# Attention with heads of 8: rounds of two steps, and each half of a step's scores issued beside a unit of the other row half

## What is computed

```python
qc, kc, vc = heads(x @ Wcq + bcq), heads(ctx @ Wck + bck), heads(ctx @ Wcv + bcv)   # 16 heads of 8
attc = einsum('bhqd,bhkd->bhqk', qc, kc) * 8 ** -0.5                                # 256 x 1601 per head
y = einsum('bhqk,bhkd->bhqd', softmax(att_causal), v)                               # first layer only
y = y + einsum('bhqk,bhkd->bhqd', softmax(attc), vc)
x = x + y.reshape(B, T, 128) @ Wp + bp                                              # input is layernorm(x)
```

## Time and profile before

| | |
|---|---|
| median of 3 runs | 7738.05 us (7690.1 to 7750.57) |
| span of the profiled execution | 7680.6 us |
| TensorE (PE) busy | 6854.6 us, 89% |
| VectorE (DVE) busy | 5897.9 us, 77% |
| ScalarE (ACT) busy | 4972.7 us, 65% |
| GpSimd (POOL) busy | 2316.8 us, 30% |
| L688, exponentials, 5248 of them | 2821.1 us busy |
| L747, reductions of wide units, 4608 of them | 3053.5 us busy |
| L625, pv, 20992 matmul records | 1615.8 us busy |

### The profile page before, as it was taken

One profiled execution on the slowest core, in us unless ns is written; L12 is line 12 of the kernel. 1 busy time (PEld: TensorE's weight loads), 2 busy tenths in 40 slices (PEclk: granted clock), 3 DMA queues, 4 the chain that ended last, 5 costly groups with the idle time before them and its releaser, 6 DMA issues. The chain is left out here.

```text
span 7680.6 us, 186325 instructions
## 1 busy us (share of the span) xinstructions
PE 6854.6 (89%) x73814; PEld 3108.2 (40%) x73814; DVE 5897.9 (77%) x12885; ACT 4972.7 (65%) x9846; POOL 2316.8 (30%) x2368
## 2 busy tenths in 40 slices
PE   6999999977999998788769999999996889999979
PEld 2333333343333333344424444444444433333335
DVE  6888888846898997788757777777774488999955
ACT  4787788834888886455446666666653168888842
POOL 1222222111211210155435555555554112212100
PEclk9999999987999999899879999999998589999989
DMA  5344444104434341100100000000001144343400
GB/s 101 86 98 94 94 91 94 44 27 84 95 78 103 81 92 44 28 18 17 40 22 10 9 8 10 6 10 9 5 5 56 28 103 99 75 103 85 85 26 12
DMA packets 319830, 417.82 MB, mean 54 GB/s; under 512 B 56533, under 2 KB 238054, under 8 KB 318969
## 3 DMA queue, kind: packets, MB, share of 16 engines
q1 hardware_dynamic: 317432, 405.36, 23.2%
q10 hardware_dynamic: 1536, 0.53, 0.0%
HBM read 225.41 MB, written 174.66 MB: 52 GB/s over the span
## 5 line engine op out<-in xcount | busy, mean ns | idle before, releaser
L688 ACT ACTIVATE a_probs<-scores_ps 128x512 f32<-128x512 f32 (+2 forms) x5248 | 2821.1, 591 | 356.9 <-PE scores_ps L608 263.7
L747 DVE TENSOR_REDUCE a_unit_max<-bank 128x1 f32<-128x512 f32 x3072 | 2003.7, 683 | 180.2 <-PE bank L595 145.3
L625 PE MATMUL bank<-a_probs,a_v_sb 128*9 128x256 f32 (+1 forms) x20992 | 1615.8, 380 | 29.3 <-ACT a_out_sb L695 20.3
L1299 ACT ACTIVATE cross_probs<-scores_ps 128x512 f32<-128x512 f32 (+1 forms) x1792 | 868.6, 571 | 590.4 <-PE scores_ps L1194 590.4
L608 PE MATMUL scores_ps<-a_stack 64*128 64x256 bf16 (+1 forms) x10496 | 1131.7, 275 | 60.9 <-ACT a_probs L688 55.9
L1381 DVE TENSOR_REDUCE cross_unit_max<-bank 128x1 f32<-128x512 f32 x1536 | 979.2, 685 | 253.3 <-PE bank L1180 250.2
L747 DVE TENSOR_REDUCE a_unit_max<-scores_ps 128x1 f32<-128x512 f32 x1536 | 1049.8, 683 | 160.4 <-PE scores_ps L595 143.1
L595 PE MATMUL bank<-a_stack 63*128 63x512 bf16 (+2 forms) x3413 | 1039.7, 372 | 7.4 <-DMA a_stack<-a_stack_dram 2.1
L1465 POOL TENSOR_TENSOR cross_added<-cross_probs 128x1024 f32<-128x1024 f32 x384 | 905.6, 2358 | 327.3 <-PE bank L1227 241.5
L608 PEld LDWEIGHTS scores_ps<-a_stack 64*128 64x128 bf16 (+1 forms) x10496 | 373.3, 96 | 991.1 <-ACT a_probs L688 831.7
L512 POOL CAST a_parts<-a_qk 128x512 bf16<-128x512 f32 (+3 forms) x225 | 117.7, 523 | 1893.8 <-ACT a_qk L707 1814.2
(11 more groups left out here) (421 smaller groups left out, 10031.3 us busy)
## 6 DMA issues: line engine op xcount, KB each, us to landing
a_stack_dram<-a_parts SPq DMA_DIRECT2D x288, 400.2 KB, 4.3
a_stack<-a_stack_dram SPq DMA_DIRECT2D x256, 348.2 KB, 8.0
a_stack<-a_stack_dram SPq DMA_DIRECT2D x128, 444.2 KB, 9.9
a_ctxT<-in_ctxT SPq DMA_DIRECT2D x48, 400.2 KB, 4.8
a_stack_dram<-a_parts SPq DMA_DIRECT2D x288, 64.0 KB, 2.4
a_stack_dram<-a_parts SPq DMA_DIRECT2D x96, 128.0 KB, 2.4
f_x<-x_after_dram SPq DMA_DIRECT2D x32, 256.0 KB, 3.3
x_after_dram<-a_res SPq DMA_DIRECT2D x48, 128.0 KB, 4.3
```

Of the source, the lines that this page charges most:

```text
L625: ins = pe.matmul(out_bank[32 * h:32 * h + V8, q0:TOK], v[0:n, e.t, 4 * e.g + h, :], A.probs[0:n, held, o + q0:o + TOK], start=(e.t == 0), ...
L688: act.activation(by_pair(A.probs[0:n, b, a * 512:(a + 1) * 512])[:, :, q0:TOK], by_pair(score_bank[(2 * e.i + a) % 3][0:n, :])[:, :, q0:TO ...
L747: ins = dve.tensor_reduce(unit_max[:, e.g % 2, qt, 2 * a + j, c:c + 1], bank[:, 0:e.s.chunks[c][1]], AX.X, ALU.max)
L1299: act.activation(probs[0:n, b, h, 0:m, :].rearrange("p m q -> p (m q)"), score_bank[h][0:n, 0:m * TOK], ACT.Exp, scale=scale).then_inc(S[" ...
```

## The change

Plan: `segment8`, which wrote one batch at a time, is replaced by `plan8`, which writes all batches in one list, in rounds of two steps. A round is, in order: scores half 0 of the even step, its exponential, its first units, the emptying of a side job of the round before (`late`), scores half 1, its exponential, its units, one side job of the kind `first` with its emptying (k_cross, v_cross), the same two halves for the odd step, then the pv of the two steps before the round (and of the even step too if it ends a quad), then `rest` (GpSimd's splits, transfers, layer norm), then at most one side job of the kind `last`, whose emptying is `late` in the next round. Window starts move by two steps (`SPACE8` 4 to 6). Units alternate their row half the other way round (`k ^ 1`), and the first unit of a half is issued between that half's two scores matmuls. `negmax` has two buffers. Scores of a half wait only for the bank of that half.

```diff
+    def evac(n, place, e):
+        done = put(n, place, "evac", e.batch)
+        done.job = e
+    def first(n, kind, b, **k):
+        e = put(n, "first", kind, b, **k)
+        evac(n, "first", e)
+    def last(n, kind, b, **k):
+        n += n % 2
+        while n in taken:
+            n += 2
+        taken[n] = kind
+        e = put(n, "last", kind, b, **k)
+        evac(n + 2, "late", e)
+        return n
...
+            n = last(stop, "turn", b, s=s, g=g)
+            put(n + 2, "late", "row", b, s=s, g=g)
...
+        for c in range(len(cross.chunks)):
+            first(ahead + 2 * c, "k_cross", b, c=c)
+            put(ahead + 2 * c, "rest", "split", b, j=c)
+        put(ahead, "rest", "ln_stats", b)
+        put(ahead, "rest", "ln_rstd", b)
+        put(ahead + 2, "rest", "ln_apply", b)
+        n = last(ahead + 4, "x_turned", b)
+        n = last(n + 2, "q", b)
...
+            first(ahead + 10 + 2 * j, "v_cross", b, j=j)
...
+            n = last(max(n + 2, done - done % 2 + 2 * (done % 2 == 0)), "quad_out", b, quad=quad)
...
+        n = last(n + 4, "heads_turned", b)
+        last(n + 2, "proj", b)
+
+    for n0 in range(-end, max(n for n, _ in at) + 2, 2):
+        core = 0 <= n0 < total
+        for half in range(2):
+            n = n0 + half
+            units = units_at.get(n, [])
+            for a in range(2):
+                mine = units[a * len(units) // 2:(a + 1) * len(units) // 2]
+                if core:
+                    s, g, t = steps[n % end]
+                    plan += [Ev("scores", s=s, g=g, t=t, i=n, part=a), Ev("exp", s=s, g=g, t=t, i=n, part=a)]
...
+                    if mine and mine[0].s.row_tile(mine[0].k) != a:
+                        plan[-2].beside = mine[0]
+                        mine[0].woven = True
+                plan += mine
+                if half == 0 and a == 0:
+                    plan += at.get((n0, "late"), [])
+            if half == 0:
+                plan += at.get((n0, "first"), [])
+        if 0 <= n0 <= total:
+            upto = n0 + int(n0 < total and steps[n0 % end][2] == steps[n0 % end][0].T - 1)
+            for i in range(gone, upto):
+                s, g, t = steps[i % end]
+                plan.append(Ev("pv", s=s, g=g, t=t, i=i))
...
+            gone = max(gone, upto)
+        plan += at.get((n0, "rest"), []) + at.get((n0, "last"), [])
```

TensorE's program:

```diff
-                    if e.i >= 1:
-                        pe.wait_ge(S["probs"], 2 * e.i - 1)
+                    a = e.part
+                    if 2 * e.i + a >= 3:
+                        pe.wait_ge(S["probs"], 2 * e.i + a - 2)
...
                     for j in range(2):
-                        for a in range(2):
-                            ins = pe.matmul(score_bank[(2 * e.i + a) % 3][0:n, j * TOK + q0:(j + 1) * TOK],
...
+                        ins = pe.matmul(score_bank[(2 * e.i + a) % 3][0:n, j * TOK + q0:(j + 1) * TOK],
...
+                        if j == 0 and e.beside:
+                            unit(e.beside)
```

More of the change, by code:

```diff
@@ L39 @@
 V8 = 9
-LAG8 = 3
 def key_tiles(nk):
@@ L243, in segment8 @@
[L243 to L253, removed]
@@ L256, in segment8, with put @@
-    if with_next:
-        for c in range(len(cross.chunks)):
[L258 to L264, removed]
+    total = BATCH * end
+    at, units_at, taken = {}, {}, {}
+    def put(n, place, kind, b, **k):
+        e = Ev(kind, **k)
+        e.batch = b
+        at.setdefault((n // 2 * 2, place), []).append(e)
+        return e
@@ L278, in segment8 @@
[L278 to L297, removed]
@@ L298, in segment8 @@
-    for e in plan:
-        e.cur = cur
-        e.batch = cur - 1 if e.kind in ("pv", "quad_out") and e.nxt else cur + 1 if e.nxt else cur
+            last(ahead + 18, "v_own", b)
+        done = base
+        n = base
+        for quad in range(QUADS * len(sources)):
+            done += sources[quad // QUADS].T
+            n = last(max(n + 2, done - done % 2 + 2 * (done % 2 == 0)), "quad_out", b, quad=quad)
+        put(base + end, "rest", "x_res", b)
+        n = last(n + 4, "heads_turned", b)
@@ L330, in schedule8 @@
             if e.kind in ("k_cross", "q", "k_own"):
-                projected[e.cur, e.c if e.kind == "k_cross" else len(cross.chunks)] = n
+                projected[e.batch, e.c if e.kind == "k_cross" else len(cross.chunks)] = n
             if e.kind == "quad_out":
@@ L346, in schedule8 @@
             e.turn = turns[e.s, e.g, e.batch] if e.t == 0 else None
-            e.free = pv_of.get(e.i - BUFS8)
-            if e.s.mask:
+            if e.s.mask and e.part == 1:
                 masked += 1
                 e.masked = masked_of[e.i] = masked
+        if e.kind == "exp":
+            e.free = pv_of.get(e.i - BUFS8)
     for e in plan:
+        if e.kind == "unit" and e.last:
+            e.read = turned_at.get(e.q - 2)
         if e.kind == "stack":
-            e.after_row = turns.get((cross, 2, e.cur))
+            e.after_row = turns.get((cross, 2, e.batch - 1))
     return plan, q
@@ L598, in program_pe @@
+            for e in plan:
+                b, made = e.batch % 2, e.batch
+                if e.kind == "unit" and not e.woven:
+                    unit(e)
                 if e.kind == "scores":
@@ L695, in program_act @@
                     act.activation(out_sb[:, quad_of(e), :], out_bank[:, 0:TOK], ACT.Copy).then_inc(S["heads_out"], 1)
-                if e.kind in SIDE8 and e.kind not in ("quad_out", "proj"):
+                if e.kind == "evac" and e.job.kind not in ("quad_out", "proj"):
+                    e = e.job
                     act.wait_ge(S["side_ps"], e.n + 1)
@@ L796, in program_pool @@
             for e in plan:
-                made = e.cur + 1
-                if e.kind == "scores":
+                made = e.batch
+                if e.kind == "scores" and e.part == 1:
                     s, b, i = e.s, e.i % BUFS8, e.i
```

193 lines of the change are left out of this document (101 added, 92 removed).

## The result

The changed kernel has a median of 8685.91 us (8634.94 to 8698.49, four runs) beside 7714.08 us (7685.33 to 7750.57) for the kernel before on the same chip: ratio 1.1249, 95% interval 1.1204 to 1.1294. The sign was forecast, the size was not: 8686 lies far above the 8060 predicted and above the range's end of 8190. About a third of the loss was foreseen, two thirds were not.

What follows compares the result with a forecast made beforehand. PE, DVE and ACT were all taken as near their limit, plain steps paced by three loops of nearly one length. 32 batches at +6.7 and 16 at +8.6 us gave +352 on 7680.6, 8033; with surroundings 8060, range 7700 to 8190.

Steps and rivals of the forecast that it cites:

- The round of two steps: Plain rounds: one longer loop through four score halves on three banks, 2.46 us a round against 2.36 before.
- The shape changes: On PE: two changes of array shape removed in each round of two steps, saving 0.18 us a round.
- rival B: PE's shape changes were the limit, everything else hidden: a1 69.8, a0 85.7 us a batch, about 7490 us; chance 0.13.
- s3's wait: Before a round's fourth score half, which waits for the first half's exponential: 0.46 us of idle PE.
- Side jobs against a late emptying: Rounds 0 to 16 of a1: `first` jobs wait for the bank the previous `last` job left, 10.3 us a batch.
- The 2.5 for the layer norm: Round 4 of a1: a `first` job waits for a bank emptied behind the layer norm's 1.55 us, about +2.5.
- The step that failed: GpSimd's splits and SyncE's stack transfers: some four steps later, with 17 steps of room, costing nothing.
- 0.2 us each: Row transfer before the second exponential, 0.52 us in ACT's queue: nothing to 0.43 each, taken as 3 x 0.2.
- The clock: Granted clock of 1.00 read from the earlier trace's a1; the sum held no term for a change in it.
- a0: The stage of 16 batches: 100.4 us a batch forecast, +8.6 over the 91.8 before.
- the 9.5 and 57.5 us: Time around the profiled span, by fastest run and by median, added to 8033 to give 8042 to 8090 us.
- The range: Whole kernel time: 7700 to 8190 us, leaving out rival B and the edges.

Runs made afterwards that it cites:

- e7: Changed kernel, rounds of two steps, with stack early, SPACE8 = 8, emptying in the job's own round, layer norm ahead, quad_out behind proj: 7855.14 us, ratio 1.0224.
- e4: Changed kernel with the layer norm's statistics and reciprocal root put before the first split in GpSimd's order: 8589.1 us.
- e3: Changed kernel with a `last` side job's bank emptied right behind the job, in the same round: 8223.72 us.
- e1: Changed kernel with x_turned and q taking their side-job slots first, so a1's stack transfers start earlier; a0's result not the reference's: 8399.94 us.
- e10: Kernel before with q, k_own, last split, writes and stack transfers each four steps later: 7920.93 us, ratio 1.0269.
- e9: Changed kernel with e7's amendments, rounds of one step and four buffers instead of two for the row of negated maxima: 7723.85 us, ratio 1.0014.
- e5: Changed kernel with only the weaving undone, a half's units behind its two scores matmuls: 8718.98 us.

## Why the prediction was right and wrong

- **The round of two steps** (2.46 us): right, 2.48 in the plain rounds shown, with each of its terms. Two 9-column pv take 1.05 us as taken over from the stage with 32.
- **The shape changes** (rival B): there are fewer, and PE's matmuls are shorter together by the 0.19 us of two pv, but s3's wait of 0.34 us takes it up. The Trainium skill, TensorEngine Tiling (Array Packing), Key Properties, says that changing the tiling mode drains the engine. The 0.19 us agree in kind; by the rule as a bound, the time of rival B, a1 would have gone to 69.8 us a batch. e7 has the fewer changes and no late emptying, and its a1 takes 74.7 against 74.4.
- **Side jobs against a late emptying** (10.3 us a batch in a1): right in kind. Over the bare 2.48 us and 0.37 for a `last` job, the rounds 0 to 16 of one batch cost 0.34, 0.34, 6.4, 0.9, 1.7, 3.1, 1.4 and 0.8, together 15.0 (rounds at the lower clock among them). The 2.5 for the layer norm is the mis-sized term: I took its 1.55 us from the earlier trace rows and left out that it waits for GpSimd's rstd behind a split, and that a reduction stands between it and quad_out's emptying. e4 gives back 3.1 to 5.0 us a batch of it in a3 and a1, with the clock; e3 takes the late emptying away and gives 11.1 in a1.
- **The step that failed:** "GpSimd's splits and SyncE's stack transfers come some four steps later but have 17 steps of room; nothing." The transfers did have the room (and in a0 they come eight steps later, not four). What I didn't ask is what they now lie beside: the row of quad 2, for which I counted 0.2 us each for its 0.52 of issue in ScalarE's queue, and no landing. It lands 8.6 us after its issue, and the scores that need it were due 8.63 - 4.57 = 4.1 us after it. Undone it returns 10.7 us a batch in a1 (e1, with some side jobs moved by it); made alone in the kernel before it costs 207 us (e10). In a1 that shift alone costs 1.3 us a batch only; what counts is how long before the row's issue the stack's first transfer goes. In one batch of a1 each it is 12.2 us in before (2246.99 and 2259.15), 6.9 in e10 (2320.70 and 2327.58) and 3.1 in the changed kernel (2294.98 and 2298.04), with waits of none, 1.4 (e10's mean) and 4.57 us.
- **The clock:** the sum left it at 1.00, as the earlier trace rows had it. Half-speed time grew by 1068 us, worth about 320 us by the two rounds above. It isn't a cause by itself: it follows the long waits (3.34 and 4.57 us in the rows above), and went when they went (e1, e3, e7). But by that estimate it doubles them: 4.7 us of wait and 5.0 of clock in e1.
- **a0:** +13.0 us a batch over the forecast. e1 doesn't move its stack and leaves it unmoved, e3 takes 7.9 off; mended in everything it still stands 5 to 10 us over before (e9, e7). The rows against the stack's transfers are one part (10 us a batch in e10, and the waits of e7), ScalarE's wait for a row buffer another (1.7, e9); the rest stays open, with the wait for VectorE's maxima (about 4 us a batch in e9) as the largest that the traces show.
- **Around the span:** the 9.5 and 57.5 us aren't what lies around a span. Each run on record is 1.7 us above its own (8698.49 against 8696.8); the rest is the spread between executions. It is under 60 us and decides nothing.
- **The range** stopped at 8190 because its upper end held only my own terms a little larger. A transfer moved past another had no entry in it, nor had the clock.

## What to carry over

When a plan is reordered, list for every moved transfer what is in flight beside it in its new place, and give each small transfer that a matmul waits for its time to landing, not its issue. In a kernel like this one, whose granted clock was 1.00, a wait of 3 to 5 us on TensorE is to be priced about twice (by the estimate above); waits of 1.4 us hardly moved the clock. And a late step in a shared bank stands in front of everything: emptying it in the same round gave back 462 us (e3), leaving the weaving out changed 33 (e5, a single run).

## What was not expected of the hardware

A transfer of 2 KB on ScalarE's queue took 8.6 us to land behind four of 348 KB on SyncE's, though it was six packets against 631 on another queue: none of the six moved until the other queue's load ran out. And the granted clock of TensorE went to its lower level behind waits of 3.3 and 4.6 us, while gaps of 0.34 us in each round left it at 1.00, and waits of 1.4 us once a batch left it there nearly always (7 us of 909 at the lower level in e10's a1).
